# Batch 1's features in the spline stage, FFN0's first batch in staggered order, turned weight tiles stored from ScalarE's queue

## The reference

```python
def spline_reconstruct(control_points, out_size, in_size):
    idx, f = _catmull_rom_grid(control_points.shape[0], out_size * in_size)
    p0, p1, p2, p3 = (control_points[idx[k]] for k in range(4))
    w = 0.5 * (2.0 * p1 + (p2 - p0) * f + (2.0 * p0 - 5.0 * p1 + 4.0 * p2 - p3) * f * f
               + (3.0 * p1 - p0 - 3.0 * p2 + p3) * f * f * f)
    return w.reshape(out_size, in_size)
gate_w, up_w = (spline_reconstruct(cp, 2048, 512) for cp in (gate_cp, up_cp))
down_w = spline_reconstruct(down_cp, 512, 2048)
gate = einsum('bsh,ih->bsi', layernorm(x), gate_w)
up = einsum('bsh,ih->bsi', layernorm(x), up_w)
x = x + tanh(g_ffn[0]) * einsum('bsi,hi->bsh', silu(gate) * up, down_w)
# FFN1's weights: q = (w / scale per 32).astype(float8_e4m3fn), times scale
```

## Time and profile before

| | us |
|---|---|
| runs | 1555.4, 1557.05, 1559.21 |
| median | 1557.05 |
| profiled execution, its own time | 1567.43 |
| its span, first to last instruction | 1565.5 |
| PE busy in it | 1309.4 (84%) |
| DVE busy | 1155.4 (74%) |
| ACT busy | 660.6 (42%) |
| POOL busy | 484.5 (31%) |

### The profile page before, as it was taken

How to read it: one execution, slowest core, us unless ns; L and a number is a source line. 1 busy time by engine, 2 the same in 40 slices (tenths; PEclk the granted TensorE clock), 3 DMA queues, 4 the chain that set the end, 5 groups by cost and what they waited for, 6 DMA issues and landing times. The chain is left out here.

```text
span 1565.5 us, 20133 instructions
## 1 busy us (share of the span) xinstructions
PE 1309.4 (84%) x7472; PEld 656.1 (42%) x7496; DVE 1155.4 (74%) x1510; ACT 660.6 (42%) x1046; POOL 484.5 (31%) x359
## 2 busy tenths in 40 slices
PE   5499998276886889986287888879999999999996
PEld 3268787123332444443022222235444444444443
DVE  5566778875566868894467777588888888888865
ACT  3434665275333444533255645224433334433322
POOL 0032342268454556642175697400000000000000
PEclk8789999558897999998599999889999999999999
DMA  8412232256133252223201102230000000000000
GB/s 306 126 59 65 80 93 64 84 192 193 64 90 119 75 152 91 81 95 137 91 1 41 28 14 82 67 121 8 7 7 7 13 7 7 7 7 13 7 8 14
DMA packets 59589, 106.50 MB, mean 68 GB/s; under 512 B 10863, under 2 KB 21767, under 8 KB 59388
## 3 DMA queue, kind: packets, MB, share of 16 engines
q1 hardware_dynamic: 58236, 101.34, 19.8%
q0 software_dynamic: 1280, 4.20, 0.9%
HBM read 73.47 MB, written 27.66 MB: 65 GB/s over the span
## 5 line engine op out<-in xcount | busy, mean ns | idle before, releaser
L1644 PE MATMUL FD<-W0D,HH 128*128 128x512 f16 x512 | 159.9, 395 | 15.4 <-DMA W0D<-down_weights,IDX 12.8
L2499 PE MATMUL HD<-W1H,HT 128*128 128x512 f16 x512 | 154.9, 379 | 0.0
L1638 PE MATMUL FG<-F,W0G 97*128 97x512 f16 x324 | 87.2, 404 | 36.8 <-ACT SG L1594 20.2
L1567 POOL TENSOR_TENSOR HL<-HM,HH 128x512 f16<-128x512 f32 x64 | 92.3, 1442 | 82.6 <-ACT HH L1596 82.3
L2302 DVE TENSOR_REDUCE NQ<-A_M 128x2 f32<-128x1024 f32 x60 | 73.3, 1222 | 50.4 <-PE A_M L2149 50.2
L335 ACT ACTIVATE DD<-E,TM 128x128 f32<-128x128 f32 x256 | 72.7, 369 | 72.4 <-PE E L431 70.9
L2445 ACT CAST OS<-SS 128x2048 f16<-128x2048 f32 x16 | 30.4, 1898 | 170.0 <-DVEq L2573 170.0
L1644 PE MATMUL FD<-W0D,HL 128*128 128x512 f16 x256 | 100.4, 392 | 0.0
L2499 PE MATMUL HD<-W1L,HT 128*128 128x512 f16 x256 | 97.0, 379 | 0.0
L2551 DVE SCALAR_TENSOR_TENSOR H<-HU,DS,SG 128x512 f32<-128x512 f32 x64 | 48.1, 751 | 63.5 <-ACT SG L2434 59.2
L2102 ACT ACTIVATE PT<-A_S,CM 128x1024 f32<-128x1024 f32 x64 | 70.9, 1112 | 56.3 <-PE A_S L2175 56.3
(11 more groups left out here) (365 smaller groups left out, 3030.5 us busy)
## 6 DMA issues: line engine op xcount, KB each, us to landing
VALP<-in_ffn_weights_dram SPq DMA_DIRECT2D x24, 512.0 KB, 3.7
VALQ<-in_ffn_weights_dram SPq DMA_DIRECT2D x24, 512.0 KB, 3.7
quantised_weights<-QQ SPq DMA_DIRECT2D x24, 512.0 KB, 2.8
X<-in_x_dram SPq DMA_DIRECT2D x8, 1024.0 KB, 6.1
W1H<-quantised_weights SPq DMA_DIRECT2D x3, 2048.0 KB, 8.0
F<-features_kept SPq DMA_DIRECT2D x16, 288.0 KB
CTX<-in_ctx_dram SPq DMA_DIRECT2D x4, 1024.0 KB, 7.1
features_kept<-XQ SPq DMA_DIRECT2D x4, 1024.0 KB, 7.0
```

The lines of the kernel that those rows point to most:

```text
L1567: pool.tensor_tensor(HL[:, i, :], HM[:, i % 2, :], HH[:, i, :], ALU.subtract).then_inc(hl_ready, 1)
L1638: last = pe.matmul(banks[t][:, :], GW[rows, t, lhs, cols], F[b % 2][rows, rhs, c, :], start=(n == 0), stop=(n == 2))
L1644: last = pe.matmul(DN[c][:, :], lhs[:, i, c * P:(c + 1) * P], W2[:, i, part, :], start=(i == 0 and n == 0), stop=(i == KI - 1 and n == 2))
L2499: ins = pe.matmul(DN[:, :], HT[:, q, lp, k, :], W[:, 2, i * D:(i + 1) * D], start=(i == 0 and lp == 0 and W is WH), stop=(i == KI - 1 and ...
```

## The change

The features of batch 1 move from FFN0's first batch into the spline stage: statistics at other units (`STATS_UNITS`), a Sqrt at unit 5, norms at units 6 and 7, transposes with high and low parts at units 9 and 11, moments at unit 14. SP writes and reads them back between the stores of NAT. Each of two batches has its own half in DRAM, its own F and its own semaphore.

In FFN0's first batch ACT does silu(i) ahead of the high part of i - 1. DVE takes the low part of i - 1 in place of POOL, which issues all 16 gathers at once. HL is turned round, so that its lower half is first written in step 8, after a wait for `nat_stored`. PE waits for the gathers in two halves.

In the stages the features of batch s + 2 are split on SP over four tiles, and `keep` moves from SP's to ACT's queue, right behind `turned`.

```diff
 MOMENT_UNIT = 3
+STATS_UNITS = (0, 1, 2, 4, 13, 15, 16, 17, 18, 19, 20, 21)
+SPREAD_UNIT = 5
+NORM_UNITS = (6, 7)
+SPLIT_UNITS = (9, 11)
+MOMENT_UNIT_1 = 14
...
+            sp.dma_start(IDX[:, :], A["class_rows"]).then_inc(idx_loaded, 16)
             for k in range(0, KI, 4):
                 sp.wait_ge(wl_ready, CLASS_UNITS + k + 4)
                 sp.dma_start(natural.rearrange("(k p) c -> p k c", p=P)[:, k:k + 4, :],
                              NAT[:, k:k + 4, :, :].rearrange("p k a c -> p k (a c)")).then_inc(nat_stored, 16)
+                if k == 0:
+                    features.keep_elements(sp, 1)
+                    features.near_elements(sp, 1)
+                elif k == 4:
+                    features.keep_moments(sp, 1)
+                    features.near_moments(sp, 1)
...
+                if u == SPREAD_UNIT:
+                    act.wait_ge(mv_ready, 2 * NC)
+                    nc.scalar.activation(SD[:, NC:2 * NC], MV[:, NC:2 * NC, 1], ACT.Sqrt, bias=EPS[:, 0:1]).then_inc(sd_ready, 1)
+                if u in SPLIT_UNITS:
+                    half = SPLIT_UNITS.index(u)
+                    if half == 0:
+                        act.wait_ge(features.xq_kept, 16)
+                    features.high(act, 1, range(2 * half, 2 * half + 2), T)
+                if u == MOMENT_UNIT_1:
+                    act.wait_ge(features.mq_kept, 16)
+                    features.high_moments(act, 1, T)
...
+                if u in SPLIT_UNITS:
+                    half = SPLIT_UNITS.index(u)
+                    features.transposes(pe, 1, range(2 * half, 2 * half + 2), T)
+                if u == MOMENT_UNIT_1:
+                    features.moments(pe, 1, T)
...
+                if u in NORM_UNITS:
+                    half = NORM_UNITS.index(u)
+                    if half == 0:
+                        v.wait_ge(sd_ready, 2)
+                        v.reciprocal(RS[:, NC:2 * NC], SD[:, NC:2 * NC]).then_inc(eps_ready, 1)
+                        v.wait_ge(eps_ready, 3)
+                    features.norm(v, 1, range(2 * half, 2 * half + 2))
+                if u in SPLIT_UNITS:
+                    half = SPLIT_UNITS.index(u)
+                    features.low(v, 1, range(2 * half, 2 * half + 2), T)
+                if u == MOMENT_UNIT_1:
+                    features.low_moments(v, 1, T)
...
-    def keep(self, sp, n):
-        sp.wait_ge(self.tw_taken, 2 * n + 2)
-        sp.dma_start(self.store[n].rearrange("a p c -> p a c"), self.Q[:, n % 2, :, :]).then_inc(self.stored[n % 2], 16)
+    def keep(self, act, n):
+        act.wait_ge(self.tw_taken, 2 * n + 2)
+        act.dma_start(self.store[n].rearrange("a p c -> p a c"), self.Q[:, n % 2, :, :]).then_inc(self.stored[n % 2], 16)
...
-                    quantiser.keep(sp, n)
-                    if n == tiles[1] and s + 2 < B:
-                        next_features(s + 2)
+                    if s + 2 < B:
+                        if n == tiles[1]:
+                            features.keep_elements(sp, s + 2)
+                        elif n == tiles[2]:
+                            sp.wait_ge(u_ready, (s + 1) * KI)
+                            features.near_elements(sp, s + 2)
+                        elif n == tiles[3]:
+                            features.keep_moments(sp, s + 2)
+                        elif n == tiles[4]:
+                            features.near_moments(sp, s + 2)
...
-            pool.wait_ge(f_loaded, 16 * F_DMAS)
             for i in range(KI):
                 pool.indirect_dma_start(W2[:, i, :, :].rearrange("p a c -> p (a c)"), None, natural,
-                                        bass.IndirectOffsetOnAxis(ap=IDX[:, i:i + 1], axis=0)).then_inc(w2_loaded, 16)
-                step(0, i)
+                                        bass.IndirectOffsetOnAxis(ap=IDX[:, i:i + 1], axis=0)).then_inc(w2_loaded[2 * i // KI], 16)
...
-                step(0, i)
+                silu(0, i)
+                if i:
+                    high(0, i - 1)
+            high(0, KI - 1)
...
                             quantiser.turned(act, n, T)
+                            quantiser.keep(act, n)
...
-            pe.wait_ge(w2_loaded, 16 * KI)
...
+                        if s == 0 and i % (KI // 2) == 0:
+                            pe.wait_ge(w2_loaded[2 * i // KI], 16 * KI // 2)
...
+            def low(i):
+                v.wait_ge(hh_ready, i + 1)
+                if i == KI // 2:
+                    v.wait_ge(nat_stored, 16 * (KI // 4))
+                v.tensor_tensor(HL[:, KI - 1 - i, :], HM[:, i % 2, :], HH[:, i, :], ALU.subtract).then_inc(hl_ready, 1)
...
                 gated(0, i)
+                if i:
+                    low(i - 1)
+            low(KI - 1)
```

More of the change, by code:

```diff
@@ L993, with spline_phase @@
 MOMENT_UNIT = 3
-def spline_phase(nc, A, X, CO, MV, RS, GW, W2, idf, scratch, natural, nat_stored, features, quantiser, used, stack):
+STATS_UNITS = (0, 1, 2, 4, 13, 15, 16, 17, 18, 19, 20, 21)
[3 more added lines that the diff above has]
+MOMENT_UNIT_1 = 14
+def spline_phase(nc, A, X, CO, MV, RS, GW, W2, idf, scratch, natural, nat_stored, IDX, idx_loaded, features, quantiser, used, stack):
     def sb(name, shape, dt=F32):
@@ L1404 @@
 MS = 0.25
+FEATURE_ROWS = D + CLASSES * 32
 class Features:
@@ L1507, in moments, with ffn0_phase @@
             last.then_inc(self.m_ready, 1)
-def ffn0_phase(nc, A, X, tg, idh, GW, W2, natural, nat_stored, features, SCL, quantiser, stack):
+def ffn0_phase(nc, A, X, tg, idh, GW, W2, natural, nat_stored, IDX, idx_loaded, features, SCL, quantiser, stack):
     def sb(name, shape, dt=F32):
@@ L1515, in ffn0_phase @@
     sem = nc.alloc_semaphore
-    features.F[1] = sb("F01", [P, 2, CLASSES, S], F16)
-    F, f_loaded = features.F, features.f_loaded
+    F = features.F
+    HL = sb("HL0", [P, KI, S], F16)
     HH = sb("HH0", [P, KI, S], F16)
-    HL = sb("HL0", [P, KI, S], F16)
     SG = sb("SG0", [P, 2, S])
@@ L1522, in ffn0_phase @@
     DS = sb("DS0", [P, 4])
-    IDX = sb("IDX", [P, INTER // P], I32)
     T, GU = ([stack.enter_context(nc.psum_tensor(f"F{n}{i}", [P, 512], F32)) for i in range(2)] for n in ("T", "G"))
     DN = [stack.enter_context(nc.psum_tensor(f"FD{i}", [P, 512], F32)) for i in range(NC)]
-    w2_loaded, idx_loaded = sem("c_w2"), sem("c_idx")
+    w2_loaded = [sem(f"c_w2{i}") for i in range(2)]
     (g_ready, u_ready, sg_ready, hm_ready, hh_ready, hl_ready, dn_ready, x_added, ds_ready) = (sem("c_" + n) for n in (
         "g", "u", "sg", "hm", "hh", "hl", "dn", "x_added", "ds"))
-    F_DMAS = WINDOWS + 1
     def pair(b, i):
@@ L1589, in _, with silu @@
         def _(act):
-            def step(b, i):
+            def silu(b, i):
                 act.wait_ge(g_ready, b * KI + i + 1)
@@ L1594, in step, with high @@
                 nc.scalar.activation(SG[:, i % 2, :], pair(b, i)[0][:, :], ACT.Silu, scale=DS[:, 0:1]).then_inc(sg_ready, 1)
+            def high(b, i):
                 act.wait_ge(hm_ready, b * KI + i + 1)
@@ L1599, in _ @@
             for i in range(KI):
-                if i == 6:
-                    features.high(act, 1, range(0, 2), T)
-                if i == 9:
-                    features.high(act, 1, range(2, 4), T)
-                if i == 12:
-                    features.high_moments(act, 1, T)
-                step(0, i)
+                silu(0, i)
+                if i:
+                    high(0, i - 1)
+            high(0, KI - 1)
             for s in range(STAGES):
@@ L1623, in _ @@
                     if s + 1 < B:
-                        step(s + 1, i)
+                        silu(s + 1, i)
+                        high(s + 1, i)
         @block.tensor
@@ L1642, in down @@
             def down(b, c, i):
-                for n, (lhs, part) in enumerate(((HH, 0), (HH, 1), (HL, 0))):
-                    last = pe.matmul(DN[c][:, :], lhs[:, i, c * P:(c + 1) * P], W2[:, i, part, :],
+                for n, (lhs, at, part) in enumerate(((HH, i, 0), (HH, i, 1), (HL, KI - 1 - i, 0))):
+                    last = pe.matmul(DN[c][:, :], lhs[:, at, c * P:(c + 1) * P], W2[:, i, part, :],
                                      start=(i == 0 and n == 0), stop=(i == KI - 1 and n == 2))
@@ L1669, in _ @@
                         if i == 0:
-                            pe.wait_ge(f_loaded, 16 * F_DMAS * (s + 2))
+                            features.in_place(pe, s + 1)
                         gate_up(s + 1, i)
@@ L1722, in _ @@
             for i in range(KI):
-                if i < NC:
-                    features.norm(v, 1, [i])
-                if i == 6:
-                    features.low(v, 1, range(0, 2), T)
-                if i == 9:
-                    features.low(v, 1, range(2, 4), T)
-                if i == 12:
-                    features.low_moments(v, 1, T)
                 gated(0, i)
+                if i:
+                    low(i - 1)
+            low(KI - 1)
             for s in range(STAGES):
@@ L2680, in build_program @@
```

(9 more changed lines are left out.)

63 lines of the change are left out of this document (26 added, 37 removed).

## The result

The kernel before took 1557.85 us (median of 5 runs, 1555.4 to 1560.66), the changed kernel 1550.62 us (5 runs, 1545.85 to 1551.28): the ratio is 0.9944 with a 95% interval of 0.9924 to 0.9964. The change is faster, but by 7 us and not by the 30 that were forecast, and 1550.6 lies above the forecast's 1514 to 1540. Measured once more (1549.56 us against 1561.6), the ratio was 0.9926 (0.9903 to 0.9948).

What follows compares the result with a forecast made beforehand. No single engine was taken to bound the kernel, but holes in the first batch (paced by POOL) and stages 0 and 1 (SP's in-order queue). Terms 16 + 20.4 - 6 = 30.4 us off 1557.05 gave 1527 us, range 1514 to 1540.

Steps and rivals of the forecast that it cites:

- Spline stage: Stage before FFN0: added features work for batch 1 lengthens it by 7.5 us, between 3.6 and 10.8.
- The forecast's own sign of being wrong: Spline stage: the forecast is wrong if this stage grows by over 11 us.
- The high end: Spline stage: all of VectorE's added work shows, six subtractions 4.1 us and four norms 6.7 us, together 10.8 us.
- First batch, shorter: FFN0's first batch: VectorE steps of 1.4 us, earlier down products and no features work; the start gains 16 us, ends 8 and 22.
- The natural weights: SP's stores of the down weights: last ones landed at 366 us, before VectorE's wait at step 8, about 371.
- Rival B: Natural weights land at 374 us, VectorE waits at step 8, start gives 8 us; 22 us less, 1535 us; chance 0.13.
- Rival A: All good ends: spline stage hides most added work, silus not late; about 42 us less, 1515 us; chance 0.16.
- SP's queue: Stages 0 to 2: features spread over four tiles and stores off SP remove ScalarE's waits, 20.4 us gained, ends 15 and 22.
- Rival C: Stages' stalls stay, raw or stored tiles late for another reason than SP's order; 10 us less, 1547 us; chance 0.08.
- Stores on ScalarE's queue: Stages 0 to 2: silus 0.5 us later in 12 of 19 steps with turned tiles, 6 us lost, ends 0 and 9.5.
- Rival D: ScalarE held until each of 19 stores lands, 2.8 us each; 17 us slower, 1574 us; chance 0.03.
- The sum: Whole kernel: 16 + 20.4 - 6 = 30.4 us less than 1557.05, giving 1527 us.

Runs made afterwards that it cites:

- h1: Changed kernel with TensorE's hooks for batch 1 later, moments in four pieces, and the features' reads back moved behind FFN0's first raw tile loads; 1542.56 us.
- h8: Changed kernel with only TensorE's later hooks for batch 1 and moments in pieces, SP's reads back left in place; ratio 0.9904 to the kernel before.
- h9: Changed kernel with only the reads back of batch 1's features moved behind FFN0's first raw tile loads; ratio 0.9917 to the kernel before.
- h5: Changed kernel with turned tiles stored from SP's queue again and the pieces of the features one or two tiles earlier; 1537.87 us.
- q3: Changed kernel with the stages' edit undone, so SP's feature steps and the stores are as before and only the new start remains; 1556.36 us.
- q2: Kernel before with the next batch's features in pieces in SP's steps, turned tiles still stored from SP, each ahead of its piece; 1550.73 us.

## Why the prediction was wrong, point by point

*Spline stage: the step that failed.* The prediction put 7.5 us on ScalarE's and VectorE's added work and costed the "32 matmuls on PE, which waits there anyway" at nothing. The stage grew by 20.1 us (44.9 to 65.0). The traces and h1, h8 and h9 divide it so: 7.3 us are those 32 products, 11.5 us at a granted clock of 0.50 less the holes that they fill; 5.8 are TensorE's waits for batch 1's norms and subtractions at its early hooks (5.6 in h8); 3.8 are the longer wait for the block's end, behind SP's reads back (3.4 of them go in h9), for which the prediction had no term; and 3.2 are VectorE's statistics and norms ahead of the eighth select. So TensorE's part, costed at nothing, was 13.1 us, and what was costed at 7.5 shows as 3.2, below its low end of 3.6. The argument from 34.7 busy of 52.8 us was an average over the stage: TensorE idles 5.4 us for batch 0's norms and subtractions, 2.5 for class selects and 5.8 at the block's end, while all of its hooks for batch 1 stand among the down units, where it waited only 0.17 us of each 1.20. The forecast's own sign of being wrong, over 11 us in this stage, came.

The high end had four norms at 1.67 us, and the Trainium skill (SBUF — State Buffer, section "SBUF: two separate sides") tells of an exclusive lock on a port pair, held for a whole instruction by whichever of VectorE and GpSimd starts first. The rows agree with the lock: two norms of 8 columns took 2.03 us beside POOL's two subtractions. They don't agree with the price: the four took 2.47 + 0.98 = 3.5 us and not 6.7, since only two of them met POOL at work.

*First batch, shorter: right.* From the first product to batch 1's first gated product the kernel before takes 103.3 - 44.9 = 58.4 us and the changed kernel 98.7 - 65.0 = 33.7, both by their second profiles: 24.7 us less, where the prediction had 16 + 7.5 = 23.5. (The first profile of the changed kernel has 41.8, with the stall.) The step is 1.48 us (forecast 1.4), the gathers 1.32 us apart on the mean (1.13). The natural weights landed 9 us late, at 375, and VectorE still did not wait for them, since its steps had begun 9 us late too. Rival B had the landing right (374 us) and the wait wrong; that it did not come is in part luck, as the longer spline stage hid it. Rival A fell with the spline stage. The start as a whole gained 4.6 us and not 16, for the spline stage's 12.6.

*SP's queue: right.* 20.4 us were forecast. With the stores back on SP (h5) stages 0 to 2 are 18.1 us shorter than in the second profile of before, 21.2 shorter than in the first, and 18.7 shorter than in q3, which has the same start. Rival C fell.

*Stores on ScalarE's queue: the mechanism right, the count too low.* I took 12 of 19 silus at 0.5 us, 6 us. It was nearly all of them: 9.6 us against h5, its high end, and 0.6 us a tile against q2, where 0.5 was forecast. Where VectorE was taken to be behind anyway, it was not. The rule of the Trainium skill (DMA: Bandwidth & Descriptors, section "Issuing engines are not separate DMA queues") was right where it spoke against the move: what gained was SP's order, which is to be had without moving a store, and the move itself lost 9.6 us. Rival D fell: ScalarE is held 0.37 us an issue.

*The sum.* With the measured terms it is 4.6 + 18.1 - 9.6 = 13.1 us, and the runs show 7.2 and 12.0 us. What is between was not traced to a place. It can lie in the other 1200 us: from stage 2's end to FFN1's first gated product the fifteen profiles have 341.7 to 348.3 us, and two profiles of one kernel differ there by 3.2 us (before) and 4.5 us (changed).

## What to carry to other kernels

Free time on an engine, read from a whole stage, does not pay for work that is put at one place in it: read the windows around the hook, the engine's clock there with them, before costing it at nothing. The hook of an in-order engine that takes another engine's result belongs at least one unit behind that engine's own hook, and in pieces no longer than its lead (5.8 us here). When an experiment thins an instruction out, read in its trace how long the thinned one took before saying that it doesn't matter. When a queue stalls, first sort its order and leave the issues where they are: an issue of 0.4 us moved to an engine that others wait for at every step is paid at every step.

## What the runs showed that I had not expected

TensorE stayed at a granted clock of 0.50 for 24 us in which it was busy 23.5 us, after a stretch in which it had waited for VectorE again and again (the last time 2.16 us, at 326.62), while in the stages of FFN0 it has 0.98 to 1.00 at 74 of 87 us busy. What separates the two wasn't tried. Two norms of 8 columns beside POOL's subtractions took nearly as long as two of 512, 2.03 against 2.47 us. And a profile can hold an 8 us stall that the next one of the same kernel has no trace of, with a releaser named that has nothing to do with it: a second profile of the unaltered kernel was worth more than the experiment on its cause.
